# Expert weights split in three pieces, loops of four tiles, and the raw weights issued by SyncE

## The reference, cut to what matters

```
def _L0_ffn_ref(x, gate_w, w_gate, w_up, w_down):
    ...
    routing_weights = jax.nn.softmax(router_logits.astype(jnp.float32), axis=-1)
    top_w, top_idx = jax.lax.top_k(routing_weights, TOP_K)
    ...
    g = jax.nn.silu(jnp.einsum('th,ehi->eti', xt, w_gate))
    u = jnp.einsum('th,ehi->eti', xt, w_up)
    y = jnp.einsum('eti,eih->eth', g * u, w_down)
    out = jnp.einsum('eth,te->th', y, full_w)
```

## Time and profile before

| | |
|---|---|
| median of three runs | 860.26 us (858.43 to 863.49) |
| profiled execution | 863.78 us, its span 862.1 us |
| granted TensorE clock, mean | 0.945 |
| PE busy | 731.4 us (85%) |
| DVE busy | 578.6 us (67%) |
| ACT busy | 436.5 us (51%) |
| POOL busy | 369.0 us (43%) |
| DMA | 179.73 MB, mean 208 GB/s |

### The profile page before, as it was taken

How to read it: one execution, slowest core, us unless ns; L and a number is a source line. 1 busy time by engine, 2 the same in 40 slices (tenths; PEclk the granted TensorE clock), 3 DMA queues, 4 the chain that set the end, 5 groups by cost and what they waited for, 6 DMA issues and landing times.

```text
span 862.1 us, 21273 instructions
## 1 busy us (share of the span) xinstructions
PE 731.4 (85%) x3655; PEld 590.7 (69%) x3656; DVE 578.6 (67%) x1464; ACT 436.5 (51%) x1021; POOL 369.0 (43%) x294
## 2 busy tenths in 40 slices
PE   7998788795554389999999999999999989989994
PEld 5554444454344378888788788888878878878883
DVE  5584665575434266777877767877787777777773
ACT  2771544254110155566655565656655665655652
POOL 1015644765447233434344443434434443443443
PEclk9998999996776699999999999999999999999998
DMA  9976644554466479999999999999999999999975
GB/s 303 369 229 253 228 160 175 228 177 181 168 227 214 144 129 211 247 217 212 208 243 200 209 224 202 197 202 251 206 212 236 226 193 227 231 205 199 198 123 73
DMA packets 174394, 179.73 MB, mean 208 GB/s; under 512 B 36864, under 2 KB 128768, under 8 KB 174368
## 3 DMA queue, kind: packets, MB, share of 16 engines
q0 software_dynamic: 30976, 73.48, 39.2%
q1 hardware_dynamic: 119248, 68.09, 30.7%
q10 hardware_dynamic: 24144, 37.89, 14.0%
HBM read 92.25 MB, written 87.13 MB: 208 GB/s over the span
## 4 chain that ended last, share of the span: by engine, by line
PE 62%; issue 12%; DVE 7%; another core or an unknown queue 5%; SPq 4%; ACT 3%; DVEq 2%; DMA 2%; ACTq 1%; POOL 1%; POOLq 0%
PE bank L1228 12%; PE bank L1229 10%; PE bank L1232 10%; PE bank L1205 4%; PE bank L1206 3%; PE bank L1207 3%; PE bank L1209 3%; PE bank L1208 3%; SPq L373 2%; PE bank L1060 2%; PE bank L1188 2%; PE bank L1189 2%; PE bank L1126 1%; PE bank L1132 1%
## 5 line engine op out<-in xcount | busy, mean ns | idle before, releaser
L465 POOL DMA_INDIRECT out_dram<-ctx_all,tile_token x144 | 233.2, 1619 | 336.7 <-ACT ctx_all L624 182.2
L1228 PE MATMUL bank<-w_hi,xT_hi 128*128 x576 | 202.5, 351 | 39.6 <-issue 26.3
L1229 PE MATMUL bank<-w_lo,xT_hi 128*128 x576 | 196.6, 341 | 0.0
L420 POOL DMA_INDIRECT x_sorted<-xn_kept,slots x112 | 116.8, 1043 | 135.8 <-issue 87.1
L1228 PEld LDWEIGHTS bank<-w_hi,xT_hi 128*128 128x128 f32 x576 | 109.6, 190 | 69.4 <-issue 66.1
L632 ACT ACTIVATE probT<-bank 128x192 f32<-128x192 f32 x144 | 47.1, 327 | 164.2 <-PE bank L1232 127.1
L1232 PE MATMUL bank<-w_hi,xT_lo 128*128 x576 | 124.5, 337 | 0.0
L961 DVE STREAM_TRANSPOSE x_all<-x_all 128x512 f32<-128x512 f32 x146 | 103.9, 711 | 30.0 <-DMA x_all<-x_sorted 20.4
L611 ACT ACTIVATE xT_hi<-x_all 128x512 fp32r<-128x512 f32 x146 | 91.5, 627 | 62.9 <-DVE x_all L961 61.6
L1229 PEld LDWEIGHTS bank<-w_lo,xT_hi 128*128 128x128 f32 x576 | 109.9, 191 | 2.8
L1232 PEld LDWEIGHTS bank<-w_hi,xT_lo 128*128 128x128 f32 x576 | 103.1, 190 | 0.0
(11 more groups left out here) (198 smaller groups left out, 1123.2 us busy)
## 6 DMA issues: line engine op xcount, KB each, us to landing
x_all<-x_sorted SPq DMA_DIRECT2D x584, 64.0 KB
w_raw<-in_w_gate_up_dram ACTq DMA_DIRECT2D x28, 768.0 KB
w_raw<-in_w_down_dram ACTq DMA_DIRECT2D x28, 512.0 KB
x_sorted<-pad_rows SPq DMA_DIRECT2D x1, 8720.0 KB, 31.3
x_all<-in_x_dram SPq DMA_DIRECT2D x8, 512.0 KB
ctx_all<-in_ctx_dram SPq DMA_DIRECT2D x8, 512.0 KB
out_dram<-x_all SPq DMA_DIRECT2D x8, 512.0 KB
w_raw<-in_w_gate_up_dram SPq DMA_DIRECT2D x4, 768.0 KB
```

The lines of the kernel that those rows point to most:

```text
L420: pool.indirect_dma_start(out=x_sorted, out_offset=bass.IndirectOffsetOnAxis(ap=to[:, u, k:k + 1], axis=0), in_=rows[:, u, :], in_offset=N ...
L465: pool.indirect_dma_start(out=out, out_offset=bass.IndirectOffsetOnAxis(ap=tile_token[:, k:k + 1], axis=0), in_=y_sb[:, i, :], in_offset=N ...
L1228: pe.matmul(out_gu, xT_hi[:, s, c * P:(c + 1) * P], gate_up(w_hi, c), start=(c == 0), stop=False)
L1229: pe.matmul(out_gu, xT_hi[:, s, c * P:(c + 1) * P], gate_up(w_lo, c), start=False, stop=False)
```

## The change

**Split in three pieces.** `w_raw`, `w_hi`, `w_lo` become separate tensors for gate/up (four pieces, two to each expert) and down (two). The next expert's first gate/up piece is due in the second tile of an expert, its second piece in the third tile, its down part in the fourth; an expert of fewer tiles does the rest in the next one's first tiles. ACT does each piece one tile ahead of DVE. How many pieces are due stands in one number per tile (`act_due`, `dve_due`, which also holds the expert), and the engine compares it with a register that counts the pieces done.

**Loops of four.** ACT and DVE run `run_quarters`: eight tiles unrolled, then a loop over four with one If. PE, GpSimd and SyncE keep the loop of eight.

**SyncE.** It keeps the row numbers in four registers, loads x of tile j + 2 and `xw` of tile j in one step, has four places for x instead of eight, freed by the transpose (`xT_ready`), and waits ahead of `xw` for GpSimd's sum of eight tiles before (`added`) and for the last `xw` on the same semaphore. DVE's copy of the token numbers (`tile_token`) is gone; GpSimd reads them in `xw`. In each step SyncE also reads `raw_due` and, if tile j - 2 is the first of an expert, issues the raw weights of the expert two further.

```diff
+            def load_w(eight, k):
+
+                if not is_before(eight, k, SLOTS):
+                    wait_apart(sp, "sp_passed", (added[k % 4], 16 * (quarter(eight, k) - 1)))
+                if not is_before(eight, k, 4):
+                    wait_apart(sp, "sp_passed", (xw_loaded[k % 4], 16 * quarter(eight, k)))
+                sp.dma_start(xw[:, k, :], rows_at(k)[:, H:RW]).then_inc(xw_loaded[k % 4], 16)
...
+            def load_coming_raw(eight, k):
+
+                sp.reg_load(raw_reg, raw_due[0:1, bass.ds(SLOTS * eight + k - RAW_BEHIND, 1)])
+                with sp.If(sp.snap(raw_reg, min_val=0, max_val=1) > 0):
+                    e = sp.snap(coming_reg, min_val=4, max_val=E - 1)
+                    wait_apart(sp, "sp_passed", (S["gu_ready"], 2 * e - 2), (S["down_ready"], e - 1), (S["raw_loaded"], 32 * e))
+                    load_raw(sp, e, sp.snap(e & 1, min_val=0, max_val=1))
+                    sp.reg_alu(coming_reg, coming_reg, 1, ALU.add)
...
             with sp.Fori(1, NT // SLOTS) as eight:
                 with sp.If(2 * eight < turns):
-                    for k in range(2, 6):
-                        load_tile(eight, k)
+                    for k in range(4):
+                        load_w(eight, k)
+                        load_x(eight, k + W_BEHIND)
+                        load_coming_raw(eight, k)
...
-            def load_coming_raw(regs):
-
-                e, h = split_at(act_e, regs)
-                with act_e.If(e > 1):
-                    with act_e.If(e < E - 2):
-                        wait_apart(act_e, "act_passed", (S["gate_up_ready"], e + 1), (S["down_ready"], e + 1), (S["raw_loaded"], 32 * e + 64))
-                        act_e.reg_alu(coming_reg, regs[1], 2, ALU.add)
-                        load_raw(act_e, act_e.snap(coming_reg, min_val=0, max_val=E - 1), h)
...
+            def split_gu_lo(gu_due, level=0):
+
+                done = dve.snap(gu_done_reg, min_val=4, max_val=2 * E)
+                with dve.If(done < gu_due):
+                    wait_apart(dve, "dve_passed", (S["gu_hi_ready"], done + 1))
+                    piece = dve.snap(done & 3, min_val=0, max_val=3)
+                    dve.tensor_tensor(gu_lo[:, bass.ds(piece, 1), :], gu_raw[:, bass.ds(piece, 1), :],
+                                      gu_hi[:, bass.ds(piece, 1), :].bitcast(F32), ALU.subtract).then_inc(S["gu_ready"], 1)
+                    dve.reg_alu(gu_done_reg, gu_done_reg, 1, ALU.add)
+                    if not level:
+                        split_gu_lo(gu_due, 1)
```

More of the change, by code:

```diff
@@ L58, in build @@
     G = 32
[L59 removed]
+    W_BEHIND, RAW_BEHIND = 2, 2
     assert TOPK == SLOTS and G * HC == P
@@ L213, in build @@
         count_done n_col_ready n_cmp_ready n_tile0_ready n_tile_ready cum_done cum_ready past_ready owner_done owner_ready
-        turn_cmp_ready turns_ready row_f_ready rows_ready split_found tables_ready
-        gate_up_hi gate_up_ready down_hi down_ready xT_ready xT_hi_ready xT_lo_ready gu_done sil_ready act_ready
+        turn_cmp_ready turns_ready row_f_ready rows_ready due_found tables_ready
+        gu_hi_ready gu_ready down_hi_ready down_ready xT_ready xT_hi_ready xT_lo_ready gu_done sil_ready act_ready
         actT_done aT_hi_ready aT_lo_ready y_done y_evac dve_passed pool_passed act_passed sp_passed""".split()
         S = {n: sem(n) for n in names}
-        xg_loaded = [sem(f"xg_loaded{i}") for i in range(SLOTS)]
+        xg_loaded = [sem(f"xg_loaded{i}") for i in range(4)]
+        xw_loaded = [sem(f"xw_loaded{i}") for i in range(4)]
         last_scattered = [sem(f"last_scattered{k}") for k in range(TOPK)]
@@ L264, in run_tiles, with run_quarters @@
             return turns
+        def run_quarters(eng, step):
+            turns = load_turns(eng)
+            for k in range(SLOTS):
+                step(k // 4, k % 4)
+            with eng.Fori(2, NT // 4) as q:
+                with eng.If(q < turns):
+                    for k in range(4):
+                        step(q, k)
         def quarter(eight, k):
@@ L272, in is_before, with tile_is_before @@
             return type(eight) is int and SLOTS * eight + k < first
+        def tile_is_before(q, k, first):
+            return type(q) is int and 4 * q + k < first
         def load_turns(eng):
@@ new lines, in _, with slot_of, transpose_x @@
+            dve.wait_ge(S["due_found"], 12)
+            dve.scalar_tensor_tensor(dve_due[:], gu_due, 32.0, expert_of[:], ALU.mult, ALU.add)
+            dve.tensor_copy(act_due[:, 0:NTX - 1], gu_due[:, 1:NTX])
+            dve.tensor_copy(raw_due[:], is_first).then_inc(S["tables_ready"], 1)
+            def slot_of(q, i):
+                return 4 * (q % 2) + i if type(q) is int else 4 * dve.snap(q & 1, min_val=0, max_val=1) + i
+            def transpose_x(q, k):
+                n, i = divmod(k, 4)
+                if not tile_is_before(q, k, 2):
+                    dve.wait_ge(S["xT_lo_ready"], 4 * q + k - 1)
+                dve.wait_ge(xg_loaded[i], 16 * HC * (q + n + 1))
+                dve.transpose(xb[:, i % 2, :].rearrange("p (c b t) -> p b c t", c=HC, b=HC),
+                              xg[:, i, :]).then_inc(S["xT_ready"], 1)
```

298 lines of the change are left out of this document (155 added, 143 removed).

## The result

The changed kernel takes 1068.22 us (median of 4 runs, 1057.95 to 1069.17), the kernel before 861.88 (median of 4, 858.43 to 875.75): a ratio of 1.238, 95% interval 1.228 to 1.249. The prediction was slower, at 938 us with a range of 887 to 985: the direction and the engine were right, the size was not. Of the 206 us that the change costs, 76 were foreseen and 130 were not.

What follows compares the result with a forecast made beforehand. PE looked like the bound at 3.47 us a tile, SyncE as full; after the change SyncE bounds at 4.45. 318 + 135 x 4.45 = 919, + 4.0 + 16.8 = 939.5, + 1.7 - 3.5 = 938 us; range 887 to 985.

Steps and rivals of the forecast that it cites:

- the sum for SyncE: SyncE's time per tile in the expert stage: today's 3.47 us plus its added work gives 4.45 us.
- Loop ends: Ends of SyncE's loop: 0.6 us per four tiles, 0.15 a tile, already within the 3.47.
- (a): SyncE's read of raw_due for every tile, with register operation and branch: 0.55 us a tile, between 0.4 and 0.9.
- (c): SyncE issuing two raw weight DMAs for each of 28 experts: 2.0 us per expert, 0.41 a tile.
- (b): SyncE's fifth DMA waiting for added and xw_loaded, with counter steps: 0.15 us a tile, between 0.1 and 0.3.
- the 0.08 for lighter traffic: SyncE's slow instructions: 0.08 us a tile taken off because a slower kernel has less traffic per us.
- The ends: Outside SyncE's loop tiles: start at 318, 4.0 us from last x to transpose, 16.8 from there to span end.
- PE's side: Smaller splits and shorter register loads on DVE and PE: worth almost 56 us if PE stayed the bound.
- The clock: PE's clock might fall as PE is less busy: given nothing of its own, only widening the upper end.
- SyncE keeps up: Rival: PE stays the bound, SyncE under 3.5 us a tile, 812 us in all; chance 0.08.
- A third of the sum: Rival: SyncE's additions come to a third, 3.85 us a tile, 857 us in all; chance 0.05.
- x behind the weights: Rival: weights ahead in the queue hold up SyncE's own DMAs, 2 us more per expert, 994 us; chance 0.09.

Runs made afterwards that it cites:

- e12: Changed kernel with a never-executed block of 64 instructions ahead of SyncE's loop: 908.3 us (kernel before, same chip, 793.1).
- e4: Changed kernel with SyncE's loop of four tiles and the due flag packed into the row number, one read a tile: 884.6 us (before, same chip, 790.4).
- e13: Changed kernel with a never-executed block of 256 instructions ahead of SyncE's loop: 987.0 us (kernel before, same chip, 793.1).
- e5: The changed kernel, unedited, on another chip: 1070.4 us (kernel before, same chip, 869.0).
- e15: Changed kernel with ScalarE issuing raw weights behind its splits, gate/up and down a tile apart: 786.0 us (kernel before, same chip, 793.1).
- e2: Changed kernel with ScalarE instead of SyncE issuing the raw weights, ahead of its splits: 834.8 us (kernel before, same chip, 790.4).
- e14: Kernel before with eight never-executed blocks of 22 in SyncE's loop, the loop moved by 60 instructions: 839.8 us (kernel before, same chip, 793.1).
- e9: Kernel before with eight never-executed blocks of 48 semaphore increments in SyncE's loop: 847.0 us (kernel before, same chip, 791.1).

## Why the prediction was wrong

**SyncE becomes the bound: right.** DVE waits for x (182.2 us), SyncE for nothing, PE's floor is untouched: 3.47 us (610.31 to 613.78) between transposes of the activations where x is there and the clock is granted in full:

```profile
604.06 0.33 PE L1255 MATMUL bank<-ident,probT 128*128 128x128 f32 x1 [3.16 <-DVE probT L1059]
610.31 0.27 PE L1255 MATMUL bank<-ident,probT 128*128 128x128 f32 x1
613.78 0.27 PE L1255 MATMUL bank<-ident,probT 128*128 128x128 f32 x1
617.26 0.27 PE L1255 MATMUL bank<-ident,probT 128*128 128x128 f32 x1
```

The 6.25 from 604.06 to 610.31 are another thing: PE, after 3.16 us of waiting, worked at a granted clock of 0.50, 1.2 GHz, for some 3 us of them (window as the earlier trace rows):

```profile
606.00:608.00 2.00, 2.00 (x7) 1.46 (x6) 1.34 (x4) 1.39 (x4) 0.00 (x0) 0.50 0.96 138
```

DVE's waits for x did not come as 0.5 to 1 us in most tiles but as 2.8 on average in 65 of them. Most of it lies behind the weights: in tiles 20 to 144 DVE waits 186 us, 117 of them in the 26 tiles whose x SyncE issued next after a pair of raw weights, and in e12, without the stalls, 92 of 103. One of them, its x issued from 593.87 on, behind weights at 591.41 and 592.05:

```profile
600.73 0.71 DVE L1011 STREAM_TRANSPOSE x_all<-x_all 128x512 f32<-128x512 f32 x1 [4.05 <-DMA x_all<-x_sorted]
```

SyncE waited once for gu_ready (0.7 us) and once for xT_ready (0.4), so none of this holds SyncE back.

**The step that failed: the sum for SyncE, 3.47 + 0.55 + 0.15 - 0.05 + 0.41 - 0.08 = 4.45.** It priced every added instruction one by one and left out the loop as a whole: that at its new length and place it has to be fetched again in each turn was put at nothing. The terms against what was measured:
- Loop ends: I took them from the kernel before, 0.15 a tile, as part of the 3.47. Moved by 192 instructions the same loop loses 5.29 - 4.68 = 0.61 us a tile to instruction fetch (in the kernel after the gaps behind the back branches are 70.4 / 128 = 0.55 a tile). 0.61 x 135 = 82 us, the larger part of the miss.
- (a) to (c) without it: 4.68 measured in e12, 4.45 forecast, 0.23 x 135 = 31 us. Plain tiles took 4.34 on average in e12, 0.87 more than the 3.47 of before, where (a), (b) and the 0.08 for lighter traffic gave 0.57. A tile without a slow instruction and without a loop end there is 3.84 to 3.94, where it was 3.10 before:

```profile
440.34 0.36 SPq L400 DMA_DIRECT2D x_all<-x_sorted  x1
441.39 1.89 SPq L391 DMA_DIRECT2D x_all<-x_sorted  x4
444.28 0.37 SPq L400 DMA_DIRECT2D x_all<-x_sorted  x1
445.23 1.89 SPq L391 DMA_DIRECT2D x_all<-x_sorted  x4
```

  By the single records (a), from the last transfer of x to the end of the branch, is 0.65 on average against 0.55, and (b), from there to the end of the second counter step, 0.25 against 0.15. The 0.08 for lighter traffic did not come: the two reads of a tile sum to 0.71 against 0.40 for the one before, and the five transfers to 1.77 against 1.67. e4 prices a read from the other side: 0.39 above two register operations, its branch not counted.
- (c), the raw weights: tiles with them took 1.6 us more in e12 (5.94), forecast 2.0. Right in kind, and too high: the second of the pair took 411 ns on SyncE in the kernel after (L318), not the 778 of the attention stage.
- 5.39 - 5.29 = 0.10 a tile, 14 us, is between e13 and the kernel after; e5, on a chip like the latter's, agrees with it within 0.02. Whether it is the chip stays open.
- The ends: start +0.8, last x to its transpose +0.2, end +2.5 us (instruction fetch as well); 3.5 us had been taken off for the median.

Together 82 + 31 + 14 + 3.5 + 3.5 = 134 against the 130 that were missing. The 4 too many come from the measure: from x tile 10 to 145 the kernel after takes (1042.73 - 318.8) / 135 = 5.36 us a tile, the fifth transfers of the window 5.39.

**PE's side: half right.** DVE's load of one value takes 306 ns at the median as forecast, PE's 303:

```profile
L1052 DVEq TENSOR_LOAD <-dve_due x144: 300/306/1205, 292.7 to 1046.5; - x144
```
```profile
L1281 PEldq TENSOR_LOAD <-experts_in x144: 297/303/1062, 264.1 to 1042.8; - x144
```

That "taking the load off ACT gains nothing" fits the kernel after, but is wrong as a general word: once SyncE is free, a tile's 2.1 us of issuing on ACT decide between 3.81 and 4.19 (e15, e2). The clock, which I gave nothing of its own, did fall: 0.83 in 450:500 against 1.00, and a mean of 0.872 over the span (0.921 in e12, 0.945 before). It made tiles of PE longer, as the 6.25 above, but since SyncE waits for nobody it did not lengthen the stage here.

**The rivals.** SyncE keeps up: no. A third of the sum: no. x behind the weights: half of it. x lands late there, as shown above, and that is bearable as forecast; SyncE's own four transfers take 2.27 us behind a pair of weights in e12 against 1.88 elsewhere, 0.4 instead of the 2 us per expert, and this is already in the 1.6 of (c). That another issuing engine matters little, as the Trainium skill has it (DMA: Bandwidth & Descriptors, Issuing engines are not separate DMA queues), does not hold here, as I had forecast: from e12 to e15, where ScalarE issues the weights, a tile apart, and takes the reads of `raw_due`, it is 0.87 us a tile, and neither has instruction packets in the stage.

## What to carry to other kernels

Sum a sequencer's work per turn as you would an engine's, and then ask whether the loop as a whole still fits: its length and its place in the program, both in instructions. Instruction packets in a stage of loops, with none in the same stage before, are the sign; a shorter loop takes them away, and if it can't be shortened, dead instructions ahead of it may. When work goes from one sequencer to another, look at what else it does in that tile, and split the work if no tile has room.

## What the runs showed that was not expected

- The same loop of 319 instructions on SyncE costs 0.6 us a tile more or less by its place alone; with 64 unexecuted instructions ahead of it the kernel takes 79 us less than with 256.
- A back branch that has to fetch takes 2.4 to 6.4 us (e14, e13), as much as 9 to 23 of SyncE's register reads of 0.28; unexecuted blocks count for length (e9).
- Raw weights ahead of x in one queue make x land late (92 of DVE's 103 us of waiting in e12); it costs nothing while SyncE is the bound, and no run here tells what it would cost otherwise.
- The part of the program ahead of the stage takes about 70 us less on some chips than on others with the stage at the same pace. Why, no run here tells.
